# Graph attention on one core: DVE operands moved to PSUM, and PE two steps ahead instead of four

## What is computed

```python
idx = jnp.concatenate([edge_index, edge_index[:, ::-1]], axis=0)
src, dst = idx[:, 0], idx[:, 1]
gl, gr = ngl[src], ngr[dst]                  # ngl = node_attr @ Wl.T, ngr = node_attr @ Wr.T; 4 heads of 16
score = (att * jax.nn.leaky_relu(gl + gr, 0.2)).sum(-1)
m = jax.ops.segment_max(score, src, num_segments=N)
ex = jnp.exp(score - m[src])
denom = jax.ops.segment_sum(ex, src, num_segments=N)
alpha = ex / (denom[src] + 1e-16)
out = jax.ops.segment_sum(gr * alpha[:, :, None], src, num_segments=N)
```

## The kernel before

| line | what DVE does | inputs |
|---|---|---|
| L1024 | z = left rows + gathered rows | PSUM, SBUF |
| L1029 | terms = rows_again * weights | SBUF, SBUF |
| L1032 | the weights beside the terms | SBUF |
| L1011 | add the sums of group 0 of step r - LAG to `acc` | SBUF, PSUM |
| L999 | one-hot rows for step q + LAG (`tensor_scalar`, bf16 in, fp32 out) | SBUF |
| L1038 | leaky = max(0.2 z, z) | SBUF, SBUF |
| L1011 | the sums of group 1 | SBUF, PSUM |
| L1044 | rest = terms - bf16(terms), after L961 | SBUF, SBUF |
| L1047 | one-hot columns of step r: iota == place | SBUF, SBUF |
| L1050 | weighed = leaky * att | SBUF, SBUF |
| L1003 | row numbers of step q + 7 into `stage`, for POOL | SBUF |
| L1056 | third part = rest - bf16(rest), after L963; frees PE | SBUF, SBUF |
| L136 | scores = sums of weighed | SBUF |

## Time and profile before

### The profile page before, as it was taken

How to read it: one execution, slowest core, us unless ns; L and a number is a source line. 1 busy time by engine, 2 the same in 40 slices (tenths; PEclk the granted TensorE clock), 3 DMA queues, 4 the chain that set the end, 5 groups by cost and what they waited for, 6 DMA issues and landing times. The chain is left out here.

```text
span 9160.2 us, 75228 instructions
## 1 busy us (share of the span) xinstructions
PE 3404.2 (37%) x15299; PEld 3019.6 (33%) x15300; DVE 4781.7 (52%) x7612; ACT 797.4 (9%) x1184; POOL 5419.6 (59%) x4913
## 2 busy tenths in 40 slices
PE   1011123444343433353444335443443333333445
PEld 1011123443333333343334334332332333333443
DVE  8999922765555564575657557563811222222222
ACT  3001000111111110110111111110200000000000
POOL 0000066777677767777777777776036777667664
PEclk9975555555555555555555555555555555555555
DMA  3000022333333333333333334337211211111211
GB/s 29 0 0 0 15 68 72 98 91 92 80 90 80 90 81 84 82 103 89 90 90 91 85 87 102 91 91 67 62 34 44 46 44 44 44 45 43 45 43 31
DMA packets 569959, 587.33 MB, mean 64 GB/s; under 512 B 300682, under 2 KB 303882, under 8 KB 569522
## 3 DMA queue, kind: packets, MB, share of 16 engines
q1 hardware_dynamic: 409122, 421.04, 15.6%
q0 software_dynamic: 156672, 160.75, 11.7%
q10 hardware_dynamic: 3984, 3.89, 0.2%
HBM read 467.65 MB, written 117.55 MB: 64 GB/s over the span
## 5 line engine op out<-in xcount | busy, mean ns | idle before, releaser
L821 POOL DMA_INDIRECT rows<-gr_table,stage x3328 | 3784.8, 1137 | 2424.2 <-DVE stage L1003 1415.9
L876 PE MATMUL bank<-gl_step,hot_t 128*128 128x64 f32 x6720 | 1564.3, 412 | 2100.1 <-issue 1454.2
L876 PEld LDWEIGHTS bank<-gl_step,hot_t 128*128 128x128 f32 x6720 | 1504.5, 327 | 2228.2 <-issue 1696.5
L1332 POOL DMA_INDIRECT message<-h_table,edge_stage x1568 | 1621.4, 1034 | 825.7 <-issue 461.8
L1359 PE MATMUL bank<-message,edge_hot 128*128 128x64 f32 x3136 | 720.4, 424 | 1462.6 <-DVE message L1404 1277.9
L1359 PEld LDWEIGHTS bank<-message,edge_hot 128*128 128x128 f32 x3136 | 683.5, 330 | 1499.5 <-DVE message L1404 1310.8
L1024 DVE TENSOR_TENSOR fore<-bank,rows 128x512 f32<-128x512 f32 x416 | 283.4, 681 | 1548.4 <-remote 821.8
L883 PE MATMUL bank<-parts,hot_sum 128*128 128x204 bf16 x3328 | 685.3, 374 | 551.2 <-issue 471.0
L883 PEld LDWEIGHTS bank<-parts,hot_sum 128*128 128x128 bf16 x3328 | 507.1, 158 | 659.7 <-issue 524.4
L1388 DVE TENSOR_TENSOR agg<-agg,bank 128x64 f32 x196 | 43.3, 221 | 1241.8 <-remote 830.1
L961 ACT CAST parts<-terms 128x544 bf16<-128x544 f32 x416 | 268.5, 645 | 2936.6 <-DVE terms L1032 1916.2
(11 more groups left out here) (257 smaller groups left out, 3435.9 us busy)
## 6 DMA issues: line engine op xcount, KB each, us to landing
place_b<-place_rows SPq DMA_DIRECT2D x422, 256.0 KB
gr_rows<-rows SPq DMA_DIRECT2D x416, 256.0 KB
rows_again<-gr_rows SPq DMA_DIRECT2D x416, 256.0 KB
rows<-gr_table,stage POOLq DMA_INDIRECT x3328
edge<-in_edge_attr SPq DMA_DIRECT2D x195, 256.0 KB
gl_step<-gl_table SPq DMA_DIRECT2D x844, 32.0 KB
message<-h_table,edge_stage POOLq DMA_INDIRECT x1568
pen_s<-pen_rows ACTq DMA_DIRECT2D x56, 64.0 KB
```

What stands on the lines that cost most here:

```text
L821: pool.indirect_dma_start(rows[k][:, g, :], None, m.gr_table[:, :], bass.IndirectOffsetOnAxis(stage[k][:, g:g + 1], 0)).then_inc(s_gath[k] ...
L876: last = pe.matmul(bank[slot % LAG][:, g * D:(g + 1) * D], hot_t[slot % LAG][:, g * P:(g + 1) * P], gl_s[slot][:, g // GROUP_TILES, :], st ...
L1332: pool.indirect_dma_start(rows[k][:, e, :], None, m.h2_table[:, :], bass.IndirectOffsetOnAxis(stage[k][:, e:e + 1], 0)).then_inc(s_gath[k] ...
```

## The change

Six things are done. The iota row and `att` are copied once into PSUM bank 5, and L1047 and L1050 read them there. The weighted terms are written into PSUM (one tensor over two adjoining banks, whose halves are banks 6 and 7), ACT rounds them from there, and what is left of them is formed in place, so that L1044 and L1056 have one input in PSUM and one in SBUF. The `rest` and `terms` tensors in SBUF go. The addition of group 1 moves from behind L1038 to in front of it. Before the terms are overwritten DVE waits for `s_parts` of its own last step. LAG becomes 2: `left` uses banks 0 and 1, `scatter` banks 2 and 3, and PE, the additions, the one-hot rows and SP's loads of blocks and block numbers all stand two steps from DVE instead of four (SP's four instead of six).

```diff
--- before.py
+++ after.py
@@ -66,7 +66,7 @@
 STEPS = GROUPS // STEP_GROUPS
 CHUNK_STEPS = STEPS // CHUNKS
 GATHER_SLOTS = 8
-LAG = 4
+LAG = 2
 PAD = GATHER_SLOTS * STEP_TILES
 SORTED_STEPS = (1 << SORT_LOG) // STEP
 FAR = 8192.0
@@ -148,7 +148,9 @@
             return whole.enter_context(nc.semaphore(name))
 
         m.sb, m.sem = sb, sem
-        m.bank = [whole.enter_context(nc.psum_tensor(f"bank{i}", [P, 512], F32)) for i in range(8)]
+        m.bank = [whole.enter_context(nc.psum_tensor(f"bank{i}", [P, 512], F32)) for i in range(6)]
+        m.pair = whole.enter_context(nc.psum_tensor("pair", [P, 1024], F32))
+        m.bank += [m.pair[:, 0:512], m.pair[:, 512:1024]]
 
         m.gr_table = nc.dram_tensor("gr_table", (N, D), F32).ap()
         m.h2_table = nc.dram_tensor("h2_table", (N, D), F32).ap()
@@ -716,11 +718,13 @@
     hot2 = [sb(f"hot_sum{k}", [P, STEP_TILES, P], BF16, ctx) for k in range(LAG)]
     fore = sb("fore", [P, SCAN], F32, ctx)
     z, leaky = (fore[:, i * SW:(i + 1) * SW].rearrange("p (g f) -> p g f", f=D) for i in range(2))
-    wide = sb("wide", [P, SW + STEP_TILES * HEADS * ACCW], F32, ctx)
-    top = wide[:, 0:SCAN]
-    weighed = wide[:, 0:SW].rearrange("p (g f) -> p g f", f=D)
-    rest = wide[:, SW:].rearrange("p (g w) -> p g w", g=STEP_TILES)
-    terms = sb("terms", [P, PAIRS, ACCW], F32, ctx)
+    top = sb("top", [P, SCAN], F32, ctx)
+    weighed = top[:, 0:SW].rearrange("p (g f) -> p g f", f=D)
+    TW = GROUP_TILES * HEADS * ACCW
+    terms = m.pair[:, :].rearrange("p (b c) -> p b c", b=STEP_GROUPS)[:, :, 0:TW]
+    terms_by_tile = terms.rearrange("p b (g w) -> p b g w", g=GROUP_TILES)
+    terms_by_pair = terms.rearrange("p b (x w) -> p b x w", w=ACCW)
+    iota_ps, att_ps = bank[5][:, 0:P], bank[5][:, P:P + D]
     parts = [sb(f"parts{k}", [P, STEP_TILES, 3, HEADS * ACCW], BF16, ctx) for k in range(LAG)]
     scores = sb("scores", [P, CHUNK_TILES, HEADS], F32, ctx)
     weights = sb("weights", [P, CHUNK_TILES, HEADS], F32, ctx)
@@ -799,9 +803,11 @@
 
     def sums_of(slot, i):
 
-        return bank[4 + slot][:, i * 3 * HEADS * ACCW:(i + 1) * 3 * HEADS * ACCW]
-
-    terms_by_tile = terms[:, :, :].rearrange("p (g h) w -> p g (h w)", h=HEADS)
+        return bank[2 + slot][:, i * 3 * HEADS * ACCW:(i + 1) * 3 * HEADS * ACCW]
+
+    def part_of(slot, w):
+
+        return parts[slot][:, :, w, :].rearrange("p (b g) w -> p b g w", b=STEP_GROUPS)
 
     def place_loads(j, k):
 
@@ -958,9 +964,9 @@
                 for k in range(U):
                     r = U * j + k - CHUNK_STEPS
                     act.wait_ge(s_terms, r + 1)
-                    nc.scalar.copy(parts[k % LAG][:, :, 0, :], terms_by_tile).then_inc(s_hi, 1)
+                    nc.scalar.copy(part_of(k % LAG, 0), terms_by_tile).then_inc(s_hi, 1)
                     act.wait_ge(s_rest, r + 1)
-                    nc.scalar.copy(parts[k % LAG][:, :, 1, :], rest[:, :, :]).then_inc(s_mid, 1)
+                    nc.scalar.copy(part_of(k % LAG, 1), terms_by_tile).then_inc(s_mid, 1)
 
             def turn(part):
                 c = part.c
@@ -990,8 +996,8 @@
         @block.vector
         def _(dve):
             chain = Chain(dve, s_chain)
-            att = m.att[:, :].unsqueeze(1).to_broadcast([P, STEP_TILES, D])
-            places = m.iota_row[:, :].unsqueeze(1).to_broadcast([P, STEP_TILES, P])
+            att = att_ps.unsqueeze(1).to_broadcast([P, STEP_TILES, D])
+            places = iota_ps.unsqueeze(1).to_broadcast([P, STEP_TILES, P])
 
             def hot_of(q, slot, place_slot, loads):
 
@@ -1026,22 +1032,25 @@
                     if part.sum:
                         weight = weights[:, bass.ds(tile, STEP_TILES), :].rearrange("p g h -> p (g h)")
                         dve.wait_ge(s_load[k % V], place_loads(j - outer, k))
-                        dve.tensor_tensor(terms[:, :, 0:DH],
-                                          rows2[k % V][:, :, :].rearrange("p g (h f) -> p (g h) f", f=DH),
-                                          weight.unsqueeze(2).to_broadcast([P, PAIRS, DH]), ALU.mult)
-                        dve.tensor_copy(terms[:, :, DH:ACCW], weight.unsqueeze(2)).then_inc(s_terms, 1)
+                        weight = weight.rearrange("p (b x) -> p b x", b=STEP_GROUPS).unsqueeze(3)
+                        at_least(dve, s_parts, r)
+                        dve.tensor_tensor(terms_by_pair[:, :, :, 0:DH],
+                                          rows2[k % V][:, :, :].rearrange("p (b g) (h f) -> p b (g h) f", f=DH, b=STEP_GROUPS),
+                                          weight.to_broadcast([P, STEP_GROUPS, PAIRS // STEP_GROUPS, DH]), ALU.mult)
+                        dve.tensor_copy(terms_by_pair[:, :, :, DH:ACCW], weight).then_inc(s_terms, 1)
                     if add:
                         accumulate(r - LAG, k % LAG, 0)
                     if part.score:
                         hot_of(q + LAG, k % LAG, (k + LAG) % V, place_loads(j, k + LAG))
+                    if add:
+                        accumulate(r - LAG, k % LAG, 1)
+                    if part.score:
                         dve.wait_ge(s_z, q + 1)
                         dve.scalar_tensor_tensor(leaky[:, :, :], z[:, :, :], SLOPE, z[:, :, :], ALU.mult,
                                                  ALU.max).then_inc(s_leaky, 1)
-                    if add:
-                        accumulate(r - LAG, k % LAG, 1)
                     if part.sum:
                         dve.wait_ge(s_hi, r + 1)
-                        dve.tensor_tensor(rest[:, :, :], terms_by_tile, parts[k % LAG][:, :, 0, :], ALU.subtract
+                        dve.tensor_tensor(terms_by_tile, terms_by_tile, part_of(k % LAG, 0), ALU.subtract
                                           ).then_inc(s_rest, 1)
                         at = m.place[:, bass.ds(r * STEP_TILES, STEP_TILES)].unsqueeze(2).to_broadcast([P, STEP_TILES, P])
                         dve.tensor_tensor(hot2[k % LAG][:, :, :], places, at, ALU.is_equal)
@@ -1053,7 +1062,7 @@
                         stage_of((k - 1) % U, q + U - 1).then_inc(s_staged, 1)
                     if part.sum:
                         dve.wait_ge(s_mid, r + 1)
-                        dve.tensor_tensor(parts[k % LAG][:, :, 2, :], rest[:, :, :], parts[k % LAG][:, :, 1, :], ALU.subtract
+                        dve.tensor_tensor(part_of(k % LAG, 2), terms_by_tile, part_of(k % LAG, 1), ALU.subtract
                                           ).then_inc(s_parts, 1)
                     if part.score:
                         dve.wait_ge(s_weighed, q + 1)
@@ -1131,6 +1140,8 @@
             for k in range(U - 1):
                 stage_of(k, k).then_inc(s_staged, 1)
             chain.link(dve.memset(m.acc[:, :, :, :], 0.0))
+            chain.link(dve.tensor_copy(iota_ps, m.iota_row[:, :]))
+            chain.link(dve.tensor_copy(att_ps, m.att[:, :]))
             dve.memset(pen_s[:, SCAN:SCAN + 1], 0.0)
             dve.memset(least[:, :, :], -BIG)
             dve.memset(latest[:, :, :], -BIG)
```

## The result

| | us |
|---|---|
| before, median of 4 runs | 9118.18 (9059.37 to 9160.0) |
| after, median of 4 runs | 9614.8 (9610.94 to 9669.0) |
| ratio after to before | 1.056, 95% interval 1.049 to 1.064 |
| span of the profiled execution of after | 9613.7 |

The changed kernel is slower by 5.6%. The forecast had 2.6%.

What follows compares the result with a forecast made beforehand. POOL's gathers were taken to bound attention. Chunks 1 to 12: 2850 + 914 + 150 + 1116 + 67 = 5097 us against 4865 (+232); with chunk 0 (+10), 9160 becomes 9402, less 70 gives 9330 us, range 8650 to 9590.

Steps and rivals of the forecast that it cites:

- What binds, and the place: Attention chunks 1 to 12: POOL sets the time, its gathers, gaps and waits making 4798 of 4865 us.
- The holds: DVE instructions with two SBUF inputs hold up POOL's gathers; operands in PSUM end most holds, saving 413 us over twelve chunks.
- The walk: Gathers followed through one DVE step by the two hold rules: five gathers in 6.78 us, 0.56 us held.
- PSUM's price for DVE: Extra time of DVE instructions reading or writing PSUM: taken as zero, upper bound 1.7 us a step.
- LAG 2: PE's 5.1 us of work, needed two steps sooner, stays hidden when fed; starved, its 24 matmuls take 66 us.
- What grows instead: In chunks 1 to 12 dense gathers starve PE, raising POOL's waits for `stage` from 402 to 1116 us.
- the fed spell after each wait: After each POOL wait the other engines run at full speed for 35 us, in which DVE does 5.1 steps, POOL 3.2.
- My two stretches: Chunk 0 and 4474:4489 before the change: gathers 1.27 and 1.36 us apart, starving within some 20 us.
- left over: Time of chunks 1 to 12 that the account of gathers, gaps and waits did not cover: 67 us.
- Rival 1: Starving comes once a chunk for its own reason, not from dense gathers; all 413 us gained, 8680 us; chance 0.32.
- Rival 2: Other engines need a given amount of POOL's time off, 2.7 us a step; waits replace holds, 9090 us; chance 0.19.
- Rival 3: LAG 2 leaves PE late even when fed, in some 200 DVE-bound steps; about 9200 us; chance 0.04.

Runs made afterwards that it cites:

- the pauses: Changed kernel with a waited-for POOL memset behind each step's eighth gather, on starving chips: 400 columns 0.971, one column 1.017 of before; 400 columns in the kernel before 1.015.
- the form with pause and lead of four: Changed kernel with a 400-column POOL memset per step and POOL at most 4 steps ahead instead of 8: 8833.8 us on a starving chip, 8625.7 on a quiet one.

## Why the prediction was right in direction and wrong in size

**What binds, and the place: right.** POOL in chunks 1 to 12.

**The holds: right.** The mean gather was to fall from 1137 to about 990 ns; 995. The 281 gathers over 2 us of chunks 1 to 12 are gone; the two that the trace still has fall in the scan of chunk 0. The held time of chunks 1 to 12 was taken as 150 us; it is 3004 - 3013 x 0.945 = 157. The walk had 0.56 us held in each DVE step. On the quiet chip it is close to that: a step takes 10.6 us, of which 8 x (1027 - 945) ns = 0.66 us is held. With it the inference of the Trainium skill (page "SBUF — State Buffer", section "Who interferes with whom") that `tensor_tensor` leaves descriptor generation alone doesn't carry over to whole gathers. The operands' move to PSUM took 142 ns off the mean gather, since with LAG 2 alone it stays at 1143 and with the addition moved back at 993. What part of the gather is held, the making of its descriptors or its reading of `stage` in SBUF, which the other rule of that section would cover, no run separates.

**PSUM's price for DVE at zero: right.** 1211 ns against the 1.21 us of L1047, 714 against 712; the unknown, writing into PSUM, 689 against the 0.68 us of L1029. The upper bound of 1.7 us a step was far off. ACT's roundings out of PSUM take 612 ns where they took 645.

**LAG 2: right as costed when fed**: 1.003 (1.000 to 1.007) with LAG alone, and on the quiet chip the changed kernel's DVE waits 9 us in all for PE. When starved the working was wrong. It had PE's 24 matmuls take 66 us, with DVE standing for them; PE's starved turn takes 23.5 us (4021.94 to 4045.48), and DVE stands although the turn that it needs is done.

**What grows instead: right in kind.** Dense gathers starve the rest, which ends when POOL is eight ahead and waits. L1030's "remote" was to rise above 822; it is 2295.

**The step that failed is the fed spell after each wait.** I took 35 us; it is 14 to 16. POOL starts again at 3999.45; DVE ends its second quick step at 4013.42 and starts the next only at 4015.50, 2.08 us late by the view. A late start about 14.0 us after POOL's restart recurs in nearly every cycle outside the scans. My two stretches had shown 15 to 20, and I moved up because of one spell of 66 us. Its gathers were no thinner: 1.42 us from start to start, against 1.40 in the first ten after a wait here (median) and 1.39 and 1.41 in the two stretches; the prediction's 1.40, 1.27 and 1.36 are lengths of stretches divided by all gathers that they touch, which comes out too low in the short ones. What it had beside them are DVE's pauses of 3.1 to 4.8 us before each step, for gathered rows; why it stayed fed, no run shows. So the spacing of gathers by itself doesn't say how long PE and DVE are fed, and the working had nothing else.

With 14 to 16 us the same working gives a cycle of 2.1 to 2.4 + 2 steps, not 7.1; the trace has four. Then 94 waits fall outside the scans, 7.8 in a chunk instead of 4.2. A second term was off the other way: such a wait is 10.4 us in the mean, not 15.1. Together 81 us a chunk outside the scan and, in the mean, 30 at it, 111, in place of 64 + 29 = 93. That the two errors partly cancel is luck. In the terms of the sum:

| chunks 1 to 12, us | forecast | measured |
|---|---|---|
| gathers alone and gaps | 2850 + 914 | 2847 + 917 |
| held up | 150 | 157 |
| waits for `stage` | 1116 | 1330 |
| left over | 67 | 99 |
| sum | 5097 | 5350 |

The waits are 214 of the 253 us by which these chunks exceed their forecast. That the span, 9613.7, lies only 212 above the forecast 9402 has another cause: the parts outside took 31.5 us less than before, where 10 more were expected. They differ by more than that from run to run. The other 73 us of the miss (9330 to 9614.8) are the 70 us that I took off because the profiled execution of the kernel before was slower than its median: that of after, 9615.7, lies at its median.

**The range** failed for a deeper reason. Its upper end, 9590, left out the fed spell's own lower bound: with 20 us the cycle has 2.95 + 2 steps, 6.1 waits of 15.1 fall in a chunk, and the same working gives about 9660. And the number and the length of the waits were treated as independent, where a wait after a shorter cycle turned out shorter.

**The rivals.** Rival 1, holds gained and PE fed: refuted on the starving chips, and exactly what happens on the quiet ones, where the change gives 288.7 us (8441.8 to 8153.1). Its 413 us were too much: they took held time from 1.80 us a step to 0.57, and there it went from 1.43 (LAG 2 alone, mean gather 1124 ns) to 0.66 (1027 ns). The rule that I set beside it (the Trainium skill, "Runtime: NRT & Kernel Launch", "Instruction fetch mechanics") has nothing by which POOL's density would matter; that agrees with the quiet chips only. The starving chip's and the quiet chip's traces of the changed kernel both have the same 159 packets in the queue of instructions, so no difference in fetched instructions shows. Rival 2, a fixed time off per step: refuted, it runs from 3.8 down to 1.9 us on the starving chips. Rival 3, PE late even when fed: refuted by LAG 2 alone and by the quiet chip's trace, in which PE costs DVE 9 us.

**What stays open.** By what the other streams are starved, and what makes a chip a starving or a quiet one. Whether it is the chip or its state at the time wasn't separated: each group of runs met one chip once. That the gathers do it on a starving chip rests on the pauses, which leave the other engines' instructions as they are. Whether they help by a lower mean rate or because a silence comes every 12 us, before the 14 us of a fed spell are over, isn't separated: between two pauses the gathers are as dense as before. And the pause of a fraction of a microsecond behind each gather, which would tell, was run on a quiet chip only. That dense gathers alone are not enough rests on the quiet chips.

## What to carry to other kernels

When a kernel's bound is one engine that others hold up, look at what the others get out of those holds before you remove them: here, on the starving chips, 1.5 us a step of held gathers was also what kept PE, DVE and SP fed most of the time. If they starve without it, try to give the time back in small even pieces (one pause of 1.1 us per step, a shorter lead) rather than let a full buffer give it in lumps: 1.7 us a step less time off, 8% of the time. And measure such a change on several chips: its effect was −3.5% on the one quiet chip where it ran unaltered and +5.6 to +6.3% on the others, and the form with pause and lead of four turned both signs round (+2.1 and −2.5%). A last one: where a profile marks idle time "issue" or "remote", look up in the program what the instruction needs and when that was done. Here this tells an ordinary wait for `parts` from an engine that stands for no visible reason.

## What the runs showed of the hardware that was not expected

- Two kinds of chips, or of states: the kernel before took 8442 and 8448 us on two, 9078, 9091 and 9192 on three, with runs of one kernel on one chip within 1.6%. On the quiet ones indirect gathers 1.25 us apart for whole chunks disturb nobody; on the others, after 14 us of them (mean 1.4 us apart), DVE starts a step late and then stands for some 22 us (10 with the lead of four) with what it needs done, PE falls to one matmul per 1.4 to 3.5 us, and SP has 8.5 us between two issues.
- DVE's stand ends 4.1 us (median of 93) after POOL has fallen silent; in one trace it ended while gathers still ran.
- A one-column memset on POOL and a wait for it, between two gathers, costs 0.9 us where the plain gap is 0.30; with 400 columns 1.39.
